# A top-2 expert layer with a shared expert: every expert over every token, or sorted token tiles in three parts

## The reference, cut to what matters

```python
def _L3_ffn_ref(x, gate_w, w1, w2, w3, w1s, w2s, w3s):
    xt = x.reshape(bs * slen, dim)
    scores = softmax(xt @ gate_w.T, axis=1)
    top_scores, sel = jax.lax.top_k(scores, 2)
    ...
    routed_in = xt[token_idx] * top_scores_sorted[:, None]
    for e in range(8):
        m = (eid == e)[:, None]
        xe = jnp.where(m, routed_in, 0.0)
        h = jax.nn.silu(xe @ w1[e]) * (xe @ w3[e])
        out_routed = out_routed + jnp.where(m, h @ w2[e], 0.0)
    hs = jax.nn.silu(xt @ w1s[0]) * (xt @ w3s[0])
    out = hs @ w2s[0]
    out = out.at[token_idx].add(out_routed)
    return out.reshape(bs, slen, dim)
...
x = x + _L3_ffn_ref(_layernorm(x, axis=-1), ...)
```

## Time and profile before

| | us |
|---|---|
| median of 3 runs | 863.67 (863.02 to 864.08) |
| the profiled execution | 869.78 |
| its span, first to last instruction | 868.0 |
| TensorE clock granted, mean | 0.927 of full |

### The profile page before, as it was taken

How to read it: one execution, slowest core, us unless ns; L and a number is a source line. 1 busy time by engine, 2 the same in 40 slices (tenths; PEclk the granted TensorE clock), 3 DMA queues, 4 the chain that set the end, 5 groups by cost and what they waited for, 6 DMA issues and landing times. The chain is left out here.

```text
span 868.0 us, 14730 instructions
## 1 busy us (share of the span) xinstructions
PE 721.9 (83%) x4784; PEld 489.9 (56%) x4784; DVE 483.2 (56%) x1392; ACT 394.7 (45%) x837; POOL 238.3 (27%) x382
## 2 busy tenths in 40 slices
PE   1587888899988778798867786899999787779998
PEld 1355666566655445465534554567777665546665
DVE  4478575777777534435566865662335345344443
ACT  2465555366665555344425565543334544222221
POOL 4345453333430350426366543100001002000000
PEclk9999998899999888799958999899999898579999
DMA  9533123322221001223372320000000200023332
GB/s 298 140 99 99 51 60 102 92 70 69 63 65 50 17 34 53 80 81 107 81 199 72 81 75 2 1 2 0 1 0 1 83 1 0 3 84 100 97 95 64
DMA packets 76320, 57.96 MB, mean 67 GB/s; under 512 B 7400, under 2 KB 70120, under 8 KB 75768
## 3 DMA queue, kind: packets, MB, share of 16 engines
q1 hardware_dynamic: 74200, 52.85, 21.6%
q0 software_dynamic: 2048, 4.20, 1.6%
HBM read 25.37 MB, written 9.24 MB: 40 GB/s over the span
## 5 line engine op out<-in xcount | busy, mean ns | idle before, releaser
L911 DVE TENSOR_REDUCE negmax<-ps 128x2 f32<-128x512 f32 x256 | 169.7, 686 | 104.2 <-PE ps L1955 102.2
L1650 ACT ACTIVATE exps<-ps 128x512 f32<-128x512 f32 x256 | 148.6, 598 | 103.4 <-PE ps L1967 98.4
L1955 PE MATMUL ps<-stack 96*128 96x256 bf16 x512 | 104.1, 298 | 35.5 <-DVE negmax L911 20.4
L1967 PE MATMUL ps<-stack 99*128 99x256 bf16 x512 | 101.3, 289 | 19.3 <-DMA stack<-maxt 16.6
L1955 PEld LDWEIGHTS ps<-stack 96*128 96x128 bf16 x512 | 48.2, 103 | 60.5 <-DVE negmax L911 35.1
L1967 PEld LDWEIGHTS ps<-stack 99*128 99x128 bf16 x512 | 44.6, 102 | 60.9 <-DMA stack<-maxt 24.2
L1983 PE MATMUL ps<-exps,values 128*32 128x256 f32 x1024 | 73.0, 402 | 1.4 <-ACT exps L1650 1.4
L2212 PEld LDWEIGHTS ps<-pack_moe,ht 128*128 128x128 f32 x512 | 62.2, 192 | 16.4 <-issue 14.6
L1286 DVE SCALAR_TENSOR_TENSOR x_sb<-ps,weights,x_sb 128x128 f32<-128x128 f32 (+1 forms) x128 | 36.0, 344 | 61.7 <-PE ps L2212 61.5
L1824 ACT ACTIVATE ht<-ps,pack_moe 128x512 f32<-128x512 f32 x64 | 43.3, 686 | 57.6 <-PE ps L2301 56.0
L2212 PE MATMUL ps<-pack_moe,ht 128*128 128x128 f32 x512 | 62.5, 275 | 0.5 <-ACT ht L1824 0.5
(11 more groups left out here) (221 smaller groups left out, 1330.1 us busy)
## 6 DMA issues: line engine op xcount, KB each, us to landing
stack<-qk_parts SPq DMA_DIRECT2D x168, 128.0 KB
stack<-weights_t SPq DMA_DIRECT2D x32, 256.0 KB, 3.2
pack_moe<-in_moe SPq DMA_DIRECT2D x1, 3076.0 KB, 14.8
outputs_moe<-y_kept SPq DMA_DIRECT2D x46, 64.0 KB
ht<-gathered SPq DMA_DIRECT2D x22, 128.0 KB
gathered<-y_kept SPq DMA_DIRECT2D x10, 256.0 KB, 3.6
pack_moe<-in_moe SPq DMA_DIRECT2D x1, 2129.0 KB
pack_moe<-in_moe SPq DMA_DIRECT2D x1, 1732.0 KB, 6.8
```

Source lines behind the costliest of these rows:

```text
L911: dve.tensor_reduce(negmax_of[b % 2][:, :, h:h + 1].rearrange("p t h -> p (t h)"), ps[:, h % 2, :].rearrange("p (t k) -> p t k", t=2), AX, ...
L1650: nc.scalar.activation(exps[:, i, :], ps[:, 2 + h % 2, :], ACT.Exp, scale=scale)\
L1955: last = pe.matmul(ps[:, h % 2, t * T:(t + 1) * T], st[0:MAXROW, h, 0, t * P:(t + 1) * P], st[0:MAXROW, h, 1, :], start=True, stop=True)
L1967: last = pe.matmul(ps[:, 2 + h % 2, t * T:(t + 1) * T], st[0:MAXROW + 3, h, 1, t * P:(t + 1) * P], st[0:MAXROW + 3, h, 0, :], start=True, ...
```

## The change

moe3 is computed like moe1, with differences. It has three parts, of 6, 6 and 4 token tiles: 19 + 19 + 15 = 53 tiles of 128 rows. The weights are applied to the rows that go in: ACT writes z times the weight to `rows_of`, two copies of a token (`scale_rows`, 12, 12 and 8 activations of 128x128), and POOL scatters those. The joins are plain additions. Part 0's norm, routing and placing stand inside steps 5 to 9 of att3, where also part 1's norm stands; POOL applies the norm now (`late_norm`). Part 1's routing follows att3, and part 2's stands beside the tiles (`LATE_BEATS`). The shared expert is dense: blocks 0 and 1 between att3 and the first tile, blocks 2 and 3 behind the last. The scratch `weights_t` and its broadcasts are gone.

```diff
-SORTED = ("moe1",)
-EXPERT = {"moe1": 768}
-PARTS = 2
+SORTED = ("moe1", "moe3")
+EXPERT = {"moe1": 768, "moe3": 384}
+PART = {"moe1": (range(0, 8), range(8, NT)), "moe3": (range(0, 6), range(6, 12), range(12, NT))}
...
+LATE_BEATS = {"turn": 2, "logits": 3, "top": 4, "exp": 4, "first": (5, 6), "second": (7, 8), "mark": 9, "rank": 9,
+              "weigh": 10, "place": (11, 12), "scale": 13, "load": 14}
+LATE_JOINS = {31: 0, 33: 1, 35: 2, 37: 3, 39: 4, 41: 5, 47: 6, 49: 7, 51: 8}
+LATE_SENDS = (None, 1, 14)
+LATE_FETCHES = (23, 42, None)
+SHARED_EARLY = 2
...
             def single_head():
-                    if step == B:
-                        apply_all("moe3", 0, GROUPS["moe3"][0])
-                    if step == B + 1:
-                        route_logits("moe3", 0)
+                    if step == 6:
+                        route_logits(nxt, 0)
+                    if step == 7:
+                        route_pick(nxt, 0, (1,))
+                    if step == 8:
+                        place_tokens(nxt, 0, 0)
+                        place_tokens(nxt, 0, 1)
+                        place_tokens(nxt, 0, 2)
+                        place_tokens(nxt, 0, 3)
...
+            def late_parts(s):
+                batch_stats(B - 1, 2)
+                route_logits(s, 1)
+                route_pick(s, 1)
+                mark_picks(s, 1)
+                multiply_shared(s, 0)
+                route_weights(s, 1)
+                for part in range(3):
+                    place_tokens(s, 1, part)
+                multiply_shared(s, 1)
+                add_shared(s, 0)
+                place_tokens(s, 1, 3)
+                add_shared(s, 1)
+                sorted_tiles(s)
+                multiply_shared(s, 2)
+                multiply_shared(s, 3)
+                add_shared(s, 2)
+                add_shared(s, 3)
+                for t in range(len(LATE_JOINS), NT):
+                    join_outputs(s, t)
...
+            def late_parts(s):
+                for t in GROUPS[s][0]:
+                    for k in range(2):
+                        send_row(s, 0, t, k)
+                late_norm(2)
+                for g in (1, 2):
+                    for t in GROUPS[s][g]:
+                        for k in range(2):
+                            send_row(s, g, t, k)
+                for t in range(NT):
+                    for k in range(2):
+                        fetch_output(s, t, k)
...
+            def scale_rows(s, g):
+                wait(act, "shared_out", s, 0, g)
+                for t in GROUPS[s][g]:
+                    for k in range(2):
+                        last = nc.scalar.activation(rows_of[:, k, t, :], z[:, t, :], ACT.Copy, scale=share[:, k, t:t + 1])
+                last.then_inc(sem["rows_scaled"], 1)
...
+            def late_parts(s):
+                open_shared(s, 0)
+                wait(pe, "x_updated", "att3", B - 1)
+                open_shared(s, 1)
+                rank_tokens(s, 1)
+                close_shared(s, 0)
+                close_shared(s, 1)
+                load_experts(s, slice(0, REGISTERS))
+                wait(pe, "x_updated", s, 1)
+                sorted_tiles(s)
+                wait(pe, "y_ready", s, 0)
+                open_shared(s, 2)
+                open_shared(s, 3)
+                close_shared(s, 2)
+                close_shared(s, 3)
```

More of the change, by code:

```diff
@@ L67 @@
              ("xg", 1), ("xb", 1), ("cg", 1), ("cb", 1)],
-    "moe3": [("router", 8), ("w1", 9 * 128), ("w3", 9 * 128), ("w2", 9 * 128)],
+    "moe3": [("router", 8), ("experts", 3072), ("shared", 384)],
 }
@@ L1016, in scale_mix_weights, with batch_stats @@
                 last.then_inc(sem["mix_scaled"], 1)
+            def batch_stats(b, last_of=None):
+                wait(dve, "x_updated", "att3", b)
+                for t in range(2 * b, 2 * b + 2):
+                    last = dve.bn_stats(stats[:, t, :], x_sb[:, t, :])
+                if last_of is not None:
+                    last.then_inc(sem["stats_taken"], 1)
+                    moments_all("moe3", last_of, PART["moe3"][last_of])
             def single_head():
-                s = "att3"
+                s, nxt = "att3", "moe3"
                 dve.wait_ge(loaded[s], 16)
@@ L1879, in turn_all @@
                         wait(pe, "zt_ready", s, 0, 0)
-                    if s in SORTED and i == 1:
+                    if s == "moe1" and i == 1:
                         wait(pe, "zt_ready", s, 0, 0)
+                    if s == "moe3" and i == 1:
+                        wait(pe, "zt_ready", s, 0, i - 1)
                     for k, t in enumerate(chunks_of(s)[i]):
```

583 lines of the change are left out of this document (313 added, 270 removed).

## The result

The changed kernel took **879.77 us** (median of 5, 877.39 to 886.44), the kernel before in the same place 863.67 (859.38 to 867.60). The ratio is **1.0186**, with a 95% interval of 1.0153 to 1.0219: slower by 16 us, where 856.2 was forecast, outside the range that ended at 873. The profiled execution is the slowest of the five (886.44 us); its span is 884.4 us, 16.4 more than the 868.0 before, whose profiled execution was likewise 6 us above its median.

The account below looks back on a forecast made before the run. PE was taken as the bound in moe3, busy 97.3 of 104 us. First turn 762.7 + 58.2 + 10.5 + 8 = 839.4, plus tail 21.1 = 860.5 against 868.0: -7.5, so 856.2 us; range 848.5 to 873.

Parts of the forecast that it names:

- The term of standstills: In moe3's tile stage, waits put down to `remote` beside indirect DMAs, as in moe1: 8 us (3 to 15).
- rival 2: No stalls in moe3's tile stage, instruction fetches stay hidden: 8 us less, 848.2; chance 0.14.
- The start of the tiles: After att3, two chains, POOL's and DVE's, end at the first tile's turn: 762.7 us (760 to 765).
- rival 4: Part 0's routing delays att3 by more than its cover; 3 us later moves everything: 859; chance 0.10.
- The beat: Interval between moe3's tiles, near the dependency loop: 1.12 us (1.03 to 1.35), 58.2 us for 52 intervals.
- The sign that was named: In the tile stage, a clock of 0.50, since waiting engines leave PE half idle, would show the prediction wrong.
- What stands between the tiles: Part 2's turns, logits, routing and scalings, and first tiles at half clock, in moe3's tile stage: 10.5 us (7 to 14).
- The tail: From the last tile's turn to the end, with 8 POOL fetches of part 2 in a chain: 21.1 us (19 to 24).
- rival 3: POOL bounds the end: an indirect DMA of 1.4 instead of 1.26 us adds to start and tail, about 860; chance 0.14.
- Rival 1: moe3's tile loop costs more than the dependency loop says: interval 1.30 us, stalls and extras 25, 872 us; chance 0.20.

Follow-up runs that it names:

- after_again: The changed kernel run again without edits, on chip 3: 846.03 us against 853.59 for the kernel before, ratio 0.9931.
- after_third: The changed kernel run once more without edits, on chip 0, also called the control: 879.82 us against 865.47 for the kernel before, ratio 1.0164.
- no_dma_2: Changed kernel without scatters of parts 1 and 2, all fetches and joins behind the tiles, chip 0: 887.4 us, kernel before 865.5.

## Why the prediction was wrong, step by step

- **The term of standstills (8, with 15 as its end) is the step that failed.** From the calm trace (after_again) to the result's the tiles take 15.6 us more (86.4 for 70.8), the tail 6.3 (28.7 for 22.4) and the start 0.7 (17.8 for 17.1 from batch 7's sum): 22.6 us, and 20.1 in after_third, where the sum had 8. Its bound was taken from moe1: 15 of 21.6 us of excess. What moe1 loses to standstills is 10.8 us (94.96 here, 84.2 on a chip without). In the tile stage alone the bound of 15 nearly held: 14.5 us between the control and `no_dma_2` (86.8 - 72.3). What it left out is all that lies outside that stage, above all between the last turn and the last y, 10.4 us instead of 4.2. The term applies wherever POOL issues DMAs, from part 0's scatters to the last fetch. That a tile of 1.2 us has less slack than one of moe1, with 1.63 us of PE work, may add to it; no run shows that.
- **Its mechanism was also misread.** The prediction took the 3.25 us of the earlier trace rows for a late instruction of ACT. `remote` means there that the profile matched no instruction to the signal; the signal itself is PE's, late, at that place as at all others. That POOL was scattering or fetching at both places was read rightly.
- That the term might be **nothing** was rival 2, at 0.14. It is what four of seven chips showed. Its sum, 15.5 us below before, was still too low: the changed kernel gained 7.6 there. No row told that both cases exist, on different chips. Without standstills the trace agrees with what the Trainium skill ("Runtime: NRT & Kernel Launch", section "Instruction fetch mechanics") says of mostly hidden fetches. With them it doesn't speak against that page, as the prediction thought, since the waits end with PE's signals.
- **The start of the tiles** (762.7): 3.0 us were allowed to att3's end and it took 5.5 on the calm chip (33.6 us from batch 3's sum to batch 7's, where 28.1 stood before) and 7.0 in the result. The 2.26 us of PE's wait in step 6 were overlooked: the second chunk's turn was costed by its matmuls, not by the copy it needs first. With it came the half clock in steps that were costed at full clock. This is rival 4 (chance 0.10), with some 3.5 us for its 3. The chain behind it was right: from batch 7's sum to the first tile 16.1 us were forecast, 17.1 measured on the calm chip, and POOL's 12 scatters of 1.26 us were the ones that decided.
- **The beat** (1.12, between 1.03 and 1.35): the median interval on the calm chip is 1.20. Right within its bounds, 0.08 low, 4 us over 52. The sign that was named, a clock of 0.50 in the tile stage, did not come: it was 0.94 there and 0.86 in the result.
- **What stands between the tiles** (10.5): on the calm chip 70.8 us from first to last turn, less 52 x 1.20, is 8.4. Two too many, with the 8 scalings at 3.1 for 2.2.
- **The tail** (21.1): 22.4 on the calm chip. Right in its mechanism: POOL's fetches are the chain. On the calm chip the fetches of part 1 ended only as the last y had landed, so rival 3 nearly came in; in the result POOL had been idle 7.54 us. Shared blocks 2 and 3 were hidden, as said.
- **Rival 1** had the right sign, and 872 for 879.8, but by a partly wrong reason and partly by luck: it had 92.6 us for the tiles (a mean interval of 1.30 and extras of 25), which took 86.4, and nothing for the tail. The mean interval in the result is 1.66 us, its median 1.3, and the median without standstills 1.2: the loop is nearly as fast as forecast, and it is interrupted.

On a chip without standstills the forecast of -7.5 us met -7.6 by luck, by errors that cancel: 8 us for standstills too many, and 2.5, 1, 2 and 1.5 too few at att3's end, the start, the tiles and the tail.

## What to carry to other kernels

A row whose idle time is put down to `remote` is a reason to measure on a second chip before a sign is forecast: here the same two kernels stand 1.6 to 1.9% apart one way in two measurements and 0.7% the other way in a third. For such a row it is worth looking up whose signal the instruction waits for, and when that signal arrived. Work that trades long matmuls for a loop of short, dependent steps beside POOL's indirect DMAs is exposed to such waits in every stage where those DMAs run, and a price taken from one stage must be asked for in all of them. A step that is moved into a pipeline is to be costed by what it waits for there (a bank, a copy), since an idle PE may take its clock with it.

## What the hardware showed

- The kernel before has medians of 862 to 866 us on chips 0, 10 and 14 and of 852 to 856 on 3, 5, 11 and 15; the changed and edited kernels have 11 to 14 waits for `remote` in moe1 on the first and none on the others. Each such wait ends with a signal of PE that is 1.5 to 6.5 us late; in a standstill the signals arrive one every 1.4 us, and ACT, DVE and POOL go on at that beat.
- The packets of the instruction queues of the changed and edited kernels are as many and as long in both (39 or 40 of 16 KB with a median of 0.96 to 1.17 us, 44 or 45 of 8 KB with 0.38 to 0.48), so it is not their transfer that is slower.
- Leaving out POOL's indirect DMAs beside the tiles, and with them the joins, took the tile stage from 86.8 to 72.3 us on such a chip and from 70.7 to 68.8 on the other kind.
- With a wait of 2.26 us on PE in step 6 the granted clock fell to 0.50 in step 6 or 7 in 13 of 14 traces; with the turn moved, it stayed at 1.00 through both steps in all five, at the same work.
